# Second mixture of experts in an eight-stage kernel: stationary gate and up weights, brought from DRAM tile by tile

## The chip, the cores and the metric

The kernel runs on one core of one Trainium2 chip. The metric is the device time of one execution in microseconds (us); the time shown for a kernel is the median of its runs. All data are 32-bit floats.

## The reference

Eight layers are added to an activation `x` of 1024 tokens with 256 features, each on a layer norm of the sum so far: an attention, a mixture of experts, a wide attention, a low-rank mixture, a retention, **the second mixture of experts**, a feature attention and a product-key MLP. Only the second mixture (`L2_ffn`) is touched in what it does:

```python
def _moe(x, Wg, W1, W3, W2):            # x: 1024 tokens x 256, 8 experts, hidden 704
    gate_logits = einsum('bsd,de->bse', x, Wg)
    gate_weights = softmax(gate_logits)
    topk_w, topk_idx = top_k(gate_weights, 2)
    topk_w = topk_w / sum(topk_w)
    combine = sum(one_hot(topk_idx, 8) * topk_w[..., None], axis=-2)
    for e in range(8):
        gate = silu(x @ W1[e])           # 256 -> 704
        val = x @ W3[e]                  # 256 -> 704
        out = out + combine[..., e:e+1] * ((gate * val) @ W2[e])   # 704 -> 256
```

## The kernel before

The program is written engine by engine. `MAKERS` gives one stage for each layer, and every engine (SP, POOL, DVE, ACT, PE) runs its part of stage 0, then of stage 1, and so on; semaphores (`after` waits, `tell` signals) order the engines. Nothing is reordered by a compiler, so the order of the lines is the order on each engine. SP issues nearly all transfers, and a wait in its list holds up every transfer behind it. A `_first` function of a stage runs ahead of the `_last` function of the stage before.

`experts(k, l, ...)` makes both mixtures: stage 1 (hidden 176, with a shared expert) and stage 5 (hidden 704, without). `shared_expert` and `LAG` tell them apart. In stage 5:

- **Routing.** PE makes the router's logits (`logits`), DVE turns them into two chosen experts for each token and sorts the 2048 (token, expert) pairs by expert into 23 tiles (`TILES`) of 128 rows; a tile holds rows of one expert alone. DVE first writes one-hot matrices (`hot`, L1018), PE multiplies them into the list of rows (L1238), DVE copies it out (L1020), PE turns it (L1242), DVE writes it as integers, `inv` (L1022). Then DVE makes the two weights of each token (L1025 to L1027) and at last `eid`, the expert of each tile (L1028 to L1030).
- **Weights.** SP loads all eight experts into the big SBUF buffer ahead of the stage: each has 1408 KB of gate and up weights (L890) and 768 KB of down weights (L891), in three groups that wait for the ends of earlier stages (`order`). Engines find a tile's expert by reading `eid` into a register (`place`, L1258).
- **Rows.** POOL gathers the 128 rows of a tile from DRAM with an indirect transfer (`fetch`, L922), four tiles ahead, and scatters the results of a tile to DRAM (`deliver`, L929). `deliver` waits until the scatter before it has landed.
- **A tile.** PE turns its rows (`turn`, L1254: 2 transposes), ACT copies them (L1154), and PE multiplies in `gate_up` (L1269): the turned rows are stationary, the weights stream, in chunks of 352 columns. ACT takes the silu of the gate half (L1162), DVE multiplies by the up half (L1047), PE turns the product (`turn_h`, L1282: 6 transposes), ACT and DVE copy it (L1169, L1053), and PE multiplies with the down weights (`down`, L1293: 6 products of 256 columns); DVE copies the result (L1060). PE shows each f32 product as two MATMUL records with a weight load each (called passes here), each transpose as one: `gate_up` has 16 passes, `down` 12, `turn` 2, `turn_h` 6.

The order on PE in stage 5 for each tile s is

```python
gate_up(s); down(s - 1); turn(s + 1); turn_h(s)
```

When the last `down` has ended, the feature attention (stage 6) begins: its `ready` waits for it, and its SP part (`sp_first`, L2118 and L2120) loads `f_keys` (2048 KB) and `f_tables` (256 KB) while the mixture is still running, after its 8th and its 16th `down`. `sp_last` (L908) then brings the scattered results back, and DVE adds them.

Of the kernel before, what the change touches and what calls it, by code (L numbers as in the profile page):

```python
# [767 lines left out]
def rank_dve(e, ch, k, mask, s, n, ra, rb):  # L768
# [16 lines left out]
            "xg0", "xg1", "xg2", "xg3", "xgt_ps", "xgt_sb", "gu_ps", "hs", "h_sb", "ht_ps", "ht_act", "ht_dve",  # L785
# [3 lines left out]
def experts(k, l, F, chunk, row, base, shared_expert, prefix):  # L789
# [4 lines left out]
    NC = F // chunk  # L794
    NB = -(-F // row)
    FP = NB * row
# [3 lines left out]
    STRIDE = WGU + WD  # L800
    at0, done0 = 8 * l, LOADED + 8 * l
    WB = k.big[:, base:base + E * STRIDE]
    U = Arena(k.big[:, 0:3384], 3384)
# [17 lines left out]
    eq = hot[:, 1, 0:3].rearrange("p t m -> p (t m)")[:, 0:TILES * E].rearrange("p (s e) -> p s e", e=E)  # L821
    A = Arena(k.big[:, low:3384], 3384 - low)
    h1, hh, hT = A.take(F), A.take(FP), A.take(NB, P)
    xgT = [A.take(KB, P) for _ in (0, 1)]
    ys = [A.take(D) for _ in range(YS)]
    if shared_expert:
        A = Arena(k.big[:, 3384:16200], 16200 - 3384)
        ring = A.take(2 * RING, D)
        hT = [hT, A.take(NB, P)]
        FS, FB = 352, (128, 128, 96)  # L830
        sg, sh = [A.take(512) for _ in (0, 1)], A.take(2, len(FB), 512)
        XN = A.take(NT, D)
        shg, shu, shd = k.sh_g, k.sh_u, k.sh_d
    else:
        XN = k.XNT.ap().rearrange("p k t -> p (k t)").rearrange("p (u d) -> p u d", d=D)
        ring = XN
        hT = [hT, hT]
# [38 lines left out]
    def sp(e):  # L876
# [9 lines left out]
        for x, d in order:  # L886
            if d:
                e.wait_ge(k.x_tile, LOADED + 8 * min(d, l))
            w = WB[:, x * STRIDE:(x + 1) * STRIDE]
            tell(e.dma_start(w[:, 0:WGU], g[prefix + "_gu"][x].rearrange("p k f -> p (k f)")), "wts", 16)  # L890
            tell(e.dma_start(w[0:row, WGU:STRIDE].rearrange("p (b d) -> p b d", d=D),  # L891
                             g[prefix + "_d"][x].rearrange("(b p) d -> p b d", p=row)), "wts", 16)
        for t in range(NT):
# [3 lines left out]
            else:  # L897
                tell(e.dma_start(to_xn[t], bc(XN[:, t], 1, 2)), "xn_st", 16)
                if t == 0:
                    tell(e.dma_start(xn_d[0:P], XN[:, 0]), "xn_st", 16)  # L900

# [52 lines left out]
    def dve(e):  # L954
# [69 lines left out]
        for d, w in ((pos[:, 0], wA), (pos[:, 1], wB)):  # L1024
            ch.step(e.tensor_tensor(CN, DM, bc(d, 2, E), ALU.is_equal))  # L1025
            ch.step(e.tensor_tensor(CN, CN, W8, ALU.mult))
            ch.step(e.tensor_reduce(w, CN, AX.X, ALU.add))  # L1027
        ch.step(e.tensor_tensor(eq, bc(bend, 1, TILES), bc(k.slot_no[:, :], 2, E), ALU.is_le))  # L1028
        ch.step(e.tensor_reduce(eidf, eq, AX.X, ALU.add))
        tell(e.tensor_scalar(eid, eidf, E - 1.0, float(STRIDE), ALU.min, ALU.mult), "eid")  # L1030
        after(e, "eid", 1)
        if FP > F:
            ch.step(e.memset(hh[:, F:FP], 0.0))
# [5 lines left out]
        def product(s):  # L1039
            after(e, "hs", s + 1)  # L1040
            if LAG and s >= 1:
                after(e, "ht_ps", s)
            if shared_expert:
                u = k.bank[:, GU[s % 2], F:2 * F]
                ins = e.tensor_tensor(hh, h1, u, ALU.mult)
            else:
                ins = e.tensor_tensor(hh[:, 0:F].rearrange("p (n c) -> p n c", n=NC),  # L1047
                                      h1.rearrange("p (n c) -> p n c", n=NC), k.bank[:, NC:2 * NC, 0:chunk], ALU.mult)
            tell(ins, "h_sb")

        def turned(s):
            after(e, "ht_ps", s + 1)
            tell(e.tensor_copy(hT[s % 2][:, 4:NB], k.bank[:, HT[0] + 1, 0:(NB - 4) * P]  # L1053
                               .rearrange("p (b m) -> p b m", m=P)), "ht_dve")
# [7 lines left out]
        for s in range(TILES):  # L1062
# [3 lines left out]
            if NB > 4:  # L1066
                turned(s)
# [64 lines left out]
    def act(e):  # L1132
# [23 lines left out]
        def gate(s):  # L1156
# [3 lines left out]
            src = k.bank[:, GU[s % 2], 0:F] if shared_expert else k.bank[:, 0:NC, 0:chunk]  # L1160
            dst = h1 if shared_expert else h1.rearrange("p (n c) -> p n c", n=NC)
            tell(e.activation(dst, src, ACT.Silu), "hs")  # L1162

        def turned(s):
            after(e, "ht_ps", s + 1)
            if s >= 1 + LAG:
                after(e, "y_ps", s - LAG)
            n = min(NB, 4)
            tell(e.copy(hT[s % 2][0:row, 0:n], k.bank[0:row, HT[s % 2], 0:n * P].rearrange("p (b m) -> p b m", m=P)),  # L1169
                 "ht_act")  # L1170
# [7 lines left out]
        if LAG:  # L1178
            rows(1)
        for s in range(TILES + LAG):  # L1180
            if s < TILES:
                gate(s)
            if s + 1 < TILES and not LAG:
                rows(s + 1)
            if s >= LAG:
                turned(s - LAG)
            if s + 2 < TILES and LAG:
# [6 lines left out]
    def pe(e):  # L1194
# [54 lines left out]
        def turn(s):  # L1249
            after(e, f"xg{s % RING}", 16 * (s // RING + 1))  # L1250
            if s >= 2 or (s >= 1 and not LAG):
# [5 lines left out]
        def place(s):  # L1257
            at[s] = e.value_load(eid[0:1, s:s + 1], min_val=0, max_val=(E - 1) * STRIDE)  # L1258

        def gate_up(s):  # L1260
            after(e, "xgt_sb", s + 1)
            if s >= 1 + LAG:
                after(e, "h_sb", s - LAG)
            elif shared_expert:
                after(e, "shy", NT - 1 + s)
            for c in range(2 * NC):
                out = bank[:, GU[s % 2], c * F:(c + 1) * F] if shared_expert else bank[:, c, 0:chunk]
                for kb in range(KB):
                    ins = e.matmul(out, xgT[s % 2][:, kb, :], WB[:, bass.ds(at[s] + (kb * 2 * F + c * chunk), chunk)],  # L1269
                                   start=kb == 0, stop=kb == KB - 1)  # L1270
                if c == 0 and s + 1 < TILES:
                    place(s + 1)
            tell(ins, "gu_ps")

        def turn_h(s):
            after(e, "h_sb", s + 1)
            if s >= 1 + LAG:
                after(e, "ht_act", s - LAG)
                if NB > 4:
                    after(e, "ht_dve", s - LAG)  # L1280
            for b in range(NB):
                ins = e.transpose(bank[0:row, HT[s % 2] + b // 4, b % 4 * P:(b % 4 + 1) * P], hh[:, b * row:(b + 1) * row],  # L1282
                                  k.ident[:, :])
            tell(ins, "ht_ps")

        def down(s):
            after(e, "ht_act", s + 1)
            if NB > 4:
                after(e, "ht_dve", s + 1)
            if s >= 1 + LAG:  # L1290
                after(e, "y_sb", s - LAG)
            for b in range(NB):
                ins = e.matmul(bank[:, Y[s % 2], 0:D], hT[s % 2][0:row, b, :],  # L1293
                               WB[0:row, bass.ds(at[s] + (WGU + b * D), D)], start=b == 0, stop=b == NB - 1)
# [1724 lines left out]
```

## Time and profile before

| | |
|---|---|
| median of 3 runs | 1110.07 us (1109.78 to 1110.41) |
| the profiled execution's own time | 1108.07 us |
| its span, first to last instruction | 1106.3 us |
| mean granted TensorE clock | 0.952 of full speed |
| PE busy | 1004.5 us, 91% of the span |
| DVE, ACT, POOL busy | 567.0, 367.5, 265.8 us |
| read from and written to DRAM | 54.72 MB, 11.40 MB |

The second mixture takes the stretch from about 566 to 805 us; its 23 tiles run from about 601 to 798 us. A busy PE means that passes are in flight, not that the array is at its peak: the time from the start of one group of passes to the start of the next is the better measure. Idle time of an engine that nobody waits for costs nothing.

### The profile page before, as it was taken

To read this page: it belongs to the slowest core of one execution; us is meant where nothing else is said; L and a number is where in the kernel's file an instruction comes from. 1 tells how busy PE (TensorE), PEld (TensorE's weight loads), DVE (VectorE), ACT (ScalarE), POOL (GpSimd) and SP (SyncE) were. 2 spreads that over 40 slices of the span, in tenths; PEclk is the share of its full clock that TensorE was granted. 3 is DMA by queue.
4 is the path that set the end of the run, shared out by engine and by line. 5 is a ranking of instruction groups with operands and counts; after the bars stand their busy time and mean duration, and the time that the engine had idled before them with its cause. 6 is when DMAs were issued, how large, how long until landed. Compare 5 with 4: busy or idle time off the path is not lost.

```text
span 1106.3 us, 17644 instructions
## 1 busy us (share of the span) xinstructions
PE 1004.5 (91%) x6722; PEld 667.7 (60%) x6722; DVE 567.0 (51%) x1286; ACT 367.5 (33%) x687; POOL 265.8 (24%) x336
## 2 busy tenths in 40 slices
PE   5888999989999999978865999999869999997989
PEld 4766599546766766667653777777623443453467
DVE  5877433455435435465474221221267878556792
ACT  3653133242122122214210222221114666745660
POOL 4431342410000000031521122221252344202350
PEclk9996999999999999989976999999958999998999
DMA  9103033211101100192054013011012200020000
GB/s 286 36 2 105 9 97 91 83 57 30 38 16 39 37 27 11 34 361 82 1 217 130 20 34 110 30 43 29 20 60 76 101 1 1 2 76 0 1 10 29
DMA packets 37432, 67.25 MB, mean 61 GB/s; under 512 B 4456, under 2 KB 27080, under 8 KB 35816
## 3 DMA queue, kind: packets, MB, share of 16 engines
q1 hardware_dynamic: 29960, 51.98, 13.9%
q0 software_dynamic: 4080, 11.15, 3.5%
q10 hardware_dynamic: 3312, 3.02, 0.8%
q8 instruction: 56, 0.92, 0.3%
q14 instruction: 24, 0.20, 0.1%
HBM read 54.72 MB, written 11.40 MB: 60 GB/s over the span
## 4 chain that ended last, share of the span: by engine, by line
PE 74%; DVE 13%; ACT 5%; DMA 3%; issue 2%; POOL 2%; SPq 0%; DVEq 0%; ACTq 0%; POOLq 0%
PE bank L354 21%; PE bank L1269 13%; PE bank L1293 7%; PE bank L1619 5%; PE bank L2341 5%; PE bank L2366 3%; PE bank L2387 3%; PE bank L1282 2%; PE bank L2836 2%; PE bank L1630 2%; PE bank L1595 2%; PE bank L2405 1%; DVE big L2623 1%; DVE big L2196 1%; ACT big L563 1%
## 5 line engine op out<-in xcount | busy, mean ns | idle before, releaser
L1269 PE MATMUL bank<-big 128*128 x552 | 147.7, 417 | 0.6 <-ACT big L1154 0.6
L354 PE MATMUL bank<-XNT,big 128*128 128x512 f32 x296 | 136.5, 609 | 6.9 <-DVE big L2576 5.4
L1269 PEld LDWEIGHTS bank<-big 128*128 128x128 f32 x552 | 98.1, 191 | 39.5 <-issue 2.3
L270 POOL TENSOR_TENSOR rstd<-ve,half 128x1 f32<-128x1 f32 x48 | 27.8, 582 | 302.7 <-DVE ve L264 302.6
L2341 PE MATMUL bank<-big,xs 32*128 32x512 f32 x256 | 89.8, 738 | 11.7 <-DVE xs L281 10.2
L354 PEld LDWEIGHTS bank<-XNT,big 128*128 128x128 f32 x296 | 55.1, 194 | 69.8 <-issue 59.1
L2196 DVE TENSOR_REDUCE big<-bank 128x2 f32<-128x512 f32 x128 | 81.9, 685 | 21.2 <-PE bank L2341 20.4
L1293 PE MATMUL bank<-big 128*128 (+1 forms) x368 | 87.2, 380 | 1.1 <-ACT big L1169 1.1
L1047 DVE TENSOR_TENSOR big<-big,bank 128x704 f32<-128x704 f32 x23 | 20.4, 889 | 124.7 <-ACT big L1162 124.7
L2287 ACT ACTIVATE big<-bank 128x1024 f32<-128x1024 f32 x64 | 64.9, 1024 | 40.2 <-PE bank L2366 39.9
L354 PE MATMUL bank<-CTXT,big 128*128 128x512 f32 (+1 forms) x192 | 67.3, 495 | 10.7 <-DMA big<-wvT 10.7
L1293 PEld LDWEIGHTS bank<-big 128*128 128x128 f32 (+1 forms) x368 | 68.0, 190 | 13.6 <-issue 1.7
L2366 PE MATMUL bank<-big 32*128 32x512 f32 x256 | 69.4, 666 | 1.4 <-POOL big L2141 1.2
L1162 ACT ACTIVATE big<-bank 128x176 f32<-128x176 f32 (+1 forms) x46 | 24.8, 538 | 136.6 <-PE bank L1269 136.6
L1619 PE MATMUL bank<-big 128*128 128x256 f32 x256 | 63.5, 393 | 1.5 <-issue 1.2
L929 POOL DMA_INDIRECT yg<-big x23 | 22.7, 986 | 150.6 <-DVE big L1060 150.6
L354 PEld LDWEIGHTS bank<-CTXT,big 128*128 128x128 f32 x192 | 33.3, 199 | 40.9 <-issue 40.8
L354 PE MATMUL bank<-big,CTXT 128*128 128x256 f32 (+1 forms) x224 | 58.0, 409 | 0.0
L1478 DVE COPY big<-bank 128x512 f32<-128x512 f32 x16 | 11.1, 691 | 88.9 <-PE bank L1604 88.9
L1526 ACT COPY big<-bank 128x1024 f32<-128x1024 f32 x16 | 16.2, 1013 | 119.1 <-PE bank L1630 119.1
L1619 PEld LDWEIGHTS bank<-big 128*128 128x128 f32 x256 | 47.0, 194 | 13.5 <-DVE X L1472 5.8
L2341 PEld LDWEIGHTS bank<-big,xs 32*128 32x128 f32 x256 | 32.0, 209 | 34.7 <-issue 18.8
(350 smaller groups left out, 1758.6 us busy)
## 6 DMA issues: line engine op xcount, KB each, us to landing
big<-m_gu SPq DMA_DIRECT2D x8, 1408.0 KB
big<-m_d SPq DMA_DIRECT2D x8, 768.0 KB
big<-a_qk SPq DMA_DIRECT2D x16, 256.0 KB, 3.0
yg<-big ACTq DMA_DIRECT2D x23, 128.0 KB, 2.0
big<-m_gu SPq DMA_DIRECT2D x8, 352.0 KB
big<-a_o SPq DMA_DIRECT2D x16, 128.0 KB, 2.1
xn<-XNT SPq DMA_DIRECT2D x8, 256.0 KB, 7.1
big<-f_keys SPq DMA_DIRECT2D x1, 2048.0 KB, 8.3
```

What stands on the lines that cost most here:

```text
L270: e.tensor_tensor(k.rstd[at % NT][:, :], k.ve[at % NT][:, :], k.half[:, 0:1], ALU.pow).then_inc(k.ln_rstd, 1)
L354: ins = e.matmul(out, a, b, start=start and n == 0, stop=stop and n == len(pairs) - 1)
L929: tell(e.indirect_dma_start(yg_d, bass.IndirectOffsetOnAxis(ap=inv[:, s:s + 1], axis=0), ys[s % YS], None), f"dv{s % YS}", 16)
L1162: tell(e.activation(dst, src, ACT.Silu), "hs")
L1269: ins = e.matmul(out, xgT[s % 2][:, kb, :], WB[:, bass.ds(at[s] + (kb * 2 * F + c * chunk), chunk)], start=kb == 0, stop=kb == KB - 1)
L1293: ins = e.matmul(bank[:, Y[s % 2], 0:D], hT[s % 2][0:row, b, :], WB[0:row, bass.ds(at[s] + (WGU + b * D), D)], start=b == 0, stop=b == NB - 1)
L1619: ins = e.matmul(bank[:, QK0 + j % 2, q * D:(q + 1) * D], cT[:, t * P:(t + 1) * P], wo[h % 2], start=True, stop=True)
L2196: e.tensor_reduce(nm[t % 2][:, b, c:c + 2 * G:G], k.bank[:, step_bank(step), :].rearrange("p (j n) -> p j n", j=2), AX.X, ALU.max, negate= ...
L2287: e.activation(pt[u % 2][:, r].rearrange("p r j n -> p r (j n)"), k.bank[:, b:b + 2, :], ACT.Exp, scale=float(G) ** -0.5).then_inc(S["ex"], 1)
L2341: e.matmul(bank[:, step_bank(step), :], k.xs[t % 2][q, b * P:(b + 1) * P], cm[t % 2][q, 2 * jp:2 * jp + 2].rearrange("p j n -> p (j n)"), ...
L2366: ins = e.matmul(bank[:, pair_banks(u, pair) + r % 2, :], cr[q, t, jp, nb * P:(nb + 1) * P], xm[t % 2][q, 2 * jp:2 * jp + 2].rearrange("p ...
L2387: ins = e.matmul(bank[r * R:(r + 1) * R, VB, jp * D:(jp + 1) * D], cv[t % 2][:, nb, r * J + 2 * jp + j], pt[u % 2][:, r, j], start=nb == 0 ...
```

## The change

For stage 5 alone:

1. **Operands change places.** In `gate_up` a block of 128 weight columns is now stationary and the turned rows (128 columns) stream: 11 blocks with 2 products each, 44 passes of 128 columns in place of 16 of 352. The output comes out already turned (hidden features on partitions). `turn_h` and the two copies behind it (L1169, L1053) are gone in this stage; silu writes `h1` and the product goes straight into `hT`. The hidden size 704 is five blocks of 128 and a half: the sixth block holds the last 64 gate columns and the last 64 up columns, so silu and product each become two instructions (640 and 128 elements a partition; the second on 64 partitions). `hT` has two buffers, and the half block of `hT` that nothing writes is cleared once. The host lays out `m5_gu` and `m5_d` to match.
2. **A transfer for each tile.** The gate and up weights aren't loaded ahead any more. SP reads `eid` for each tile into a register and loads that expert's 1408 KB into one of three slots: 23 transfers in place of 8. The load of tile 1 waits for the gather of tile 1; from tile 3 on, a load waits for the end of the `gate_up` three tiles back.
3. **Down weights.** All eight (768 KB each) are loaded after one wait, for the end of stage 2, in place of three groups that wait for stages 1, 2 and 4.
4. **Order.** On PE a tile becomes `gate_up(s); down(s - 1); turn(s + 2)`, with two turned tiles made ahead of the loop and two sets of three PSUM banks for `gate_up`.
5. **Expert table.** DVE makes `eid` and the two token weights between the one-hot matrices and the copy of the list of rows, not behind it. This is done in both mixtures.
6. SP's load of `f_keys` and `f_tables` stands behind the 23 new transfers in SP's list.

```diff
-    h1, hh, hT = A.take(F), A.take(FP), A.take(NB, P)
+    if shared_expert:
+        h1, hh = A.take(F), A.take(F)
+    else:
+        h1 = A.take(WHOLE, P)
+    hT = [A.take(NB, P) for _ in (0, 1)]
...
-        GU, HT, Y, XT = (0, 0), (4, 4), (6, 6), (7, 7)
+        GU, Y, XT = (0, 3), (6, 6), (7, 7)
...
+    def gates_up(s):
+        b = GU[s % 2]
+        return k.bank[:, b:b + 3, :].rearrange("p b (n m) -> p (b n) m", m=P)
...
-        order = [(x, 0) for x in range(E)] if shared_expert else \
-            [(x, d) for d, group in ((2, (3, 4)), (3, (1, 2, 5)), (5, (0, 6, 7))) for x in group]
+        if not shared_expert:
+            e.wait_ge(k.x_tile, LOADED + 8 * min(3, l))
...
+        if shared_expert:
+            return
+        after(e, "eid", 1)
+        for s in range(TILES):
+            x = e.value_load(eid[0:1, s:s + 1], min_val=0, max_val=E - 1)
+            if s == 1:
+                after(e, "xg1", 16)
+            if s >= SLOTS:
+                after(e, "gu_ps", s - SLOTS + 1)
+            tell(e.dma_start(gu_slot[s % SLOTS], g[prefix + "_gu"][bass.ds(x, 1)].rearrange("x p k f -> p (x k f)")),
+                 f"gl{s % SLOTS}", 16)
...
         for q in (0, 1):
             tell(e.tensor_tensor(hot[:, q], bc(pr[:, q], 2, P), bc(k.row_no[:, :], 1, NT), ALU.is_equal), "hot")
+        ch.step(e.tensor_tensor(eq, bc(bend, 1, TILES), bc(k.slot_no[:, :], 2, E), ALU.is_le))
+        ch.step(e.tensor_reduce(eidf, eq, AX.X, ALU.add))
+        tell(e.tensor_scalar(eid, eidf, E - 1.0, float(STRIDE) if shared_expert else 1.0, ALU.min, ALU.mult), "eid")
+        for d, w in ((pos[:, 0], wA), (pos[:, 1], wB)):
...
         after(e, "inv_ps", 1)
...
+                gu, rest = gates_up(s), hT[s % 2][P - PART:P, WHOLE]
+                e.tensor_tensor(hT[s % 2][:, 0:WHOLE], h1, gu[:, 12 - WHOLE:12], ALU.mult)
+                tell(e.tensor_tensor(rest, rest, gu[P - PART:P, WHOLE], ALU.mult), "h_sb")
...
+                e.activation(h1, gu[:, 0:WHOLE], ACT.Silu)
+                tell(e.activation(hT[s % 2][P - PART:P, WHOLE], gu[0:PART, WHOLE], ACT.Silu), "hs")
...
         def gate_up(s):
             after(e, "xgt_sb", s + 1)
-            if s >= 1 + LAG:
-                after(e, "h_sb", s - LAG)
+            if s >= 2:
+                after(e, "h_sb", s - 1)
...
+                gu = gates_up(s)
+                after(e, f"gl{s % SLOTS}", 16 * (s // SLOTS + 1))
+                for n in range(2 * F // P):
+                    for kb in range(KB):
+                        c = kb * 2 * F + n * P
+                        ins = e.matmul(gu[:, n if n <= WHOLE else n + 1], gu_slot[s % SLOTS][:, c:c + P],
+                                       xgT[s % 2][:, kb, :], start=kb == 0, stop=kb == KB - 1)
+                    if n == 0 and s + 1 < TILES:
+                        place(s + 1)
...
         if not shared_expert:
             turn(0)
+            turn(1)
         for s in range(TILES + 1 + LAG):
...
-            if s + 1 + LAG < TILES:
-                turn(s + 1 + LAG)
-            if not LAG and s < TILES:
-                turn_h(s)
+            if s + 2 < TILES:
+                turn(s + 2)
```

## Rows read from the trace of the kernel before

**Rows 1.** The page: busy time, granted clock in 40 slices of 27.7 us.

```profile
PE 1004.5 (91%) x6722; PEld 667.7 (60%) x6722; DVE 567.0 (51%) x1286; ACT 367.5 (33%) x687; POOL 265.8 (24%) x336
...
PEclk9996999999999999989976999999958999998999
```

**Rows 2.** PE's waits, 600 to 800 us: total us, times, longest.

```profile
PE bank L1254 <- DMA XNT<-xn,big: 3.6, 1, 3.6
PE bank L1282 <- DVE big L1047: 1.6, 1, 1.6
```

**Rows 3.** Timeline of one tile: start us, us, engine, line, what.

```profile
619.21 5.00 PE L1269 MATMUL bank<-big 128*128 x16
...
624.04 2.75 PE L1293 MATMUL bank<-big 128*128 x12
624.25 0.76 ACT L1162 ACTIVATE big<-bank 128x704 f32<-128x704 f32 x1 [4.30 <-PE bank L1269]
625.04 0.89 DVE L1047 TENSOR_TENSOR big<-big,bank 128x704 f32<-128x704 f32 x1 [5.26 <-ACT big L1162]
...
626.63 0.38 PE L1254 MATMUL bank<-ident,XNT 128*128 128x128 f32 x2
...
626.85 0.82 PE L1282 MATMUL bank<-ident,big 128*128 128x128 f32 x6
...
627.57 5.00 PE L1269 MATMUL bank<-big 128*128 x16
```

**Rows 4.** Timeline of PE in the low-rank mixture: 64 passes of 128 columns.

```profile
502.36 0.61 PE L1785 MATMUL bank<-CTXT,big 128*128 128x128 f32 x4
...
504.15 0.71 PE L1785 MATMUL bank<-CTXT,big 128*128 128x128 f32 x4
504.70 0.61 PE L1787 MATMUL bank<-big,CTXT 128*128 128x128 f32 x4
...
509.83 0.38 PE L1795 MATMUL bank<-ident,big 128*128 128x128 f32 x2
```

**Rows 5.** Windows: busy us of engines, granted clock, DMA share, GB/s.

```profile
601.70:605.30 3.60, 3.59 (x7) 2.13 (x8) 0.00 (x0) 1.17 (x1) 1.63 (x2) 0.53 0.44 109
...
620.00:780.00 160.00, 160.00 (x690) 118.16 (x689) 33.03 (x57) 32.64 (x57) 36.44 (x38) 1.00 0.15 47
```

**Rows 6.** Timeline of the mixture's start, 596 to 611 us.

```profile
596.47 0.28 DVE L1020 COPY big<-bank 23x128 f32<-23x128 f32 x1 [4.73 <-PE bank L1238]
...
597.17 0.22 DVE L1025 TENSOR_TENSOR big<-big 128x64 f32<-128x64 f32 x1
...
598.90 0.99 POOL L922 DMA_INDIRECT XNT<-xn,big  x1 [0.30 <-issue]
...
599.48 0.40 DVE L1030 TENSOR_SCALAR big<-big 128x23 int32<-128x23 f32 x1
...
600.67 0.43 PE L1254 MATMUL bank<-ident,XNT 128*128 128x128 f32 x2 [3.63 <-DMA XNT<-xn,big]
...
601.71 6.69 PE L1269 MATMUL bank<-big 128*128 x16 [0.60 <-ACT big L1154]
...
610.96 4.90 PE L1269 MATMUL bank<-big 128*128 x16
```

**Rows 7.** Transfers: one load of 2048 KB, a window inside it, gathers beside it.

```profile
big<-f_keys SPq DMA_DIRECT2D x1, 2048.0 KB, 8.3
...
680.00:683.00 3.00, 3.00 (x13) 2.00 (x12) 0.00 (x0) 0.28 (x1) 0.00 (x0) 1.00 0.99 416
...
DMA to landing us min/median/max: 3.1/4.8/6.4
```

**Rows 8.** Timeline of the last tile: the last `down`, the last scatter.

```profile
795.28 2.85 PE L1293 MATMUL bank<-big 128*128 x12 [0.76 <-ACT big L1169]
...
798.87 0.97 POOL L929 DMA_INDIRECT yg<-big  x1 [3.30 <-DVE big L1060]
```

**Rows 9.** Line 1258 on PE's sequencer: reading `eid`, ns min/median/max.

```profile
L1258 PEldq TENSOR_LOAD <-big x46: 297/300/485, 140.1 to 778.1; - x46
```

More of the change, by code:

```diff
@@ L799, in experts @@
     WGU, WD = KB * 2 * F, NB * D
-    STRIDE = WGU + WD
+    STRIDE = WD + WGU * shared_expert
     at0, done0 = 8 * l, LOADED + 8 * l
     WB = k.big[:, base:base + E * STRIDE]
+    SLOTS = 3
+    gu_slot = [k.big[:, base + E * WD + q * WGU:base + E * WD + (q + 1) * WGU] for q in range(SLOTS)]
     U = Arena(k.big[:, 0:3384], 3384)
@@ L828, in experts @@
         ring = A.take(2 * RING, D)
-        hT = [hT, A.take(NB, P)]
         FS, FB = 352, (128, 128, 96)
@@ L883, in sp @@
             tell(e.dma_start(gw, g[prefix + "_gate"]), "gate_ld", 16)
[L884 to L888 removed]
+        if not shared_expert:
+            e.wait_ge(k.x_tile, LOADED + 8 * min(3, l))
+        for x in range(E):
             w = WB[:, x * STRIDE:(x + 1) * STRIDE]
[L890 to L891 removed]
+            if shared_expert:
+                tell(e.dma_start(w[:, 0:WGU], g[prefix + "_gu"][x].rearrange("p k f -> p (k f)")), "wts", 16)
+            tell(e.dma_start(w[0:row, STRIDE - WD:STRIDE].rearrange("p (b d) -> p b d", d=D),
                              g[prefix + "_d"][x].rearrange("(b p) d -> p b d", p=row)), "wts", 16)
@@ L1022, in dve @@
         tell(e.tensor_copy(inv, k.bank[:, INV, P:P + TILES]), "inv")
[L1024 to L1033, printed above, removed]
+        if not shared_expert:
+            for p in (0, 1):
+                ch.step(e.memset(hT[p][0:PART, WHOLE], 0.0))
         if shared_expert:
@@ L1040, in product @@
             after(e, "hs", s + 1)
-            if LAG and s >= 1:
-                after(e, "ht_ps", s)
             if shared_expert:
-                u = k.bank[:, GU[s % 2], F:2 * F]
-                ins = e.tensor_tensor(hh, h1, u, ALU.mult)
-            else:
[L1047 to L1054, printed above, removed]
+                if s >= 1:
+                    after(e, "ht_ps", s)
+                tell(e.tensor_tensor(hh, h1, k.bank[:, GU[s % 2], F:2 * F], ALU.mult), "h_sb")
+            else:
+                gu, rest = gates_up(s), hT[s % 2][P - PART:P, WHOLE]
+                e.tensor_tensor(hT[s % 2][:, 0:WHOLE], h1, gu[:, 12 - WHOLE:12], ALU.mult)
+                tell(e.tensor_tensor(rest, rest, gu[P - PART:P, WHOLE], ALU.mult), "h_sb")
         def result(s):
@@ L1159, in gate @@
                 after(e, "h_sb", s)
-            src = k.bank[:, GU[s % 2], 0:F] if shared_expert else k.bank[:, 0:NC, 0:chunk]
-            dst = h1 if shared_expert else h1.rearrange("p (n c) -> p n c", n=NC)
-            tell(e.activation(dst, src, ACT.Silu), "hs")
+            if shared_expert:
+                tell(e.activation(h1, k.bank[:, GU[s % 2], 0:F], ACT.Silu), "hs")
+            else:
+                gu = gates_up(s)
+                e.activation(h1, gu[:, 0:WHOLE], ACT.Silu)
+                tell(e.activation(hT[s % 2][P - PART:P, WHOLE], gu[0:PART, WHOLE], ACT.Silu), "hs")
         def turned(s):
             after(e, "ht_ps", s + 1)
-            if s >= 1 + LAG:
[L1167 to L1170, printed above, removed]
+            if s >= 2:
+                after(e, "y_ps", s - 1)
+            tell(e.copy(hT[s % 2][0:row], k.bank[0:row, HT[s % 2], 0:NB * P].rearrange("p (b m) -> p b m", m=P)), "ht_act")
         def store(s):
@@ L1177, in act @@
         rows(0)
-        if LAG:
-            rows(1)
+        rows(1)
         for s in range(TILES + LAG):
@@ L1182, in act @@
                 gate(s)
[L1183 to L1187, printed above, removed]
+            if LAG and s >= 1:
+                turned(s - 1)
+            if s + 2 < TILES:
                 rows(s + 2)
@@ L1250, in turn @@
             after(e, f"xg{s % RING}", 16 * (s // RING + 1))
-            if s >= 2 or (s >= 1 and not LAG):
+            if s >= 1 + LAG:
                 after(e, "xgt_sb", s - LAG)
```

71 lines of the change are left out of this document (36 added, 35 removed).

## The prediction

> **What bounds the kernel now.** I read the page first: PE is busy in 91% of the span [rows 1], so the question is what PE does in the stretch that is changed. PE's waits there come next. Over the 200 us of the mixture's tiles they are four, with 6.6 us together; the two longest stand in [rows 2], and all lie in the first and the last tile. The window from 620 to 780 us says the same: 160.00 of 160 us busy, granted clock 1.00, DMA engines busy in 0.15 of the time, DVE 33 us, ACT 33 us, POOL 36 us [rows 5]. PE alone sets the pace, and every other engine and the transfers have wide room. The timeline of one tile then prices PE's work by the distance of starts [rows 3]: `gate_up` 619.21 to 624.04, 4.83 us; `down` 2.59 us; `turn` 0.22 us; `turn_h` 0.72 us; 8.36 us a tile, 23 times.
>
> **The operands change places.** `turn_h` goes: 0.72 us a tile. The copies behind it go from ACT and DVE, which had idle time anyway, so they give nothing by themselves. `gate_up` keeps its product of columns and passes (16 x 352 = 44 x 128 = 5632), but needs 44 weight loads in place of 16, each hidden only behind a pass of 128 columns. The nearest rows are the 64 passes of the low-rank mixture, with a new 128x128 stationary operand at each and 128 streamed columns [rows 4]. From 502.36 to 504.15 are 16 passes: 0.112 us each. Over all 64, to 509.83, it is 0.117 us. The difference is holes of 0.10 us: the group at 504.15 takes 0.55 us to the next start where the others take 0.45. Such a hole is one pass whose weight load stood exposed because PE had just been released from a wait. I take 0.112, as the new order lets every wait of a tile be met long before (below): 44 x 0.112 = 4.92 us, so `gate_up` costs 0.09 us more than now. Bounds: 0.117 us gives 5.13, and 0.107 us (16 passes of 352 columns in 4.83 us, by column) gives 4.72.
>
> The new tile is 4.92 + 2.59 + 0.22 = 7.73 us, 0.63 us less. The clock stays at its higher level, 2.4 GHz, in this loop, since PE has even fewer gaps.
>
> **Trainium skill against this row.** The page "TensorE: Matmul & The Clock Gate", section "Measured speedup vs the span model", says that a weight load overlaps passes in flight only when it goes to another row group; here all 128 rows are used by every pass. By that rule each of the 44 loads would stand exposed: a tile of about 12.1 us and a time near 1197. The trace disagrees: an exposed load costs 0.10 us [rows 4], and most of the 64 passes show none.
>
> **Silu and product** become two instructions each. They took 0.76 and 0.89 us for 704 elements [rows 3]. If each of the four took as long as the old one, the chain would be 3.3 us; by size I take 2.4 us from the end of `gate_up` to `h_sb`. Until `down(s)` stand `down(s-1)`, `turn` and `gate_up(s+1)` on PE, 7.7 us, so it is hidden; only in the last tile is the cover no more than one `down`, 2.59 us. There I take 0, at worst 1.0 us. All the other waits (`xgt_sb`, `y_sb`, the second `gate_up` bank set) were met a tile before.
>
> **Reading `eid` on PE** stays once a tile, but now behind 4 passes of 0.112 us, not of 0.30 us. It takes 0.30 us for the load [rows 9] and some 0.2 for what follows. If PE's sequencer runs ahead of the array, which nothing now stops at `gate_up`'s head, it is hidden. If not, it costs some 0.15 us and an exposed load of 0.10 in each tile: 5.8 us in all. I take 0 and keep 5.8 for the range.
>
> **A load for each tile.** The row for a load is `f_keys`: 2048 KB landed after 8.3 us, at 416 GB/s inside [rows 7]. By size that is 5.7 us for 1408 KB; with all but the transfer itself fixed it is 3.5 + 3.3 = 6.8 us. A load is issued when `gate_up` of three tiles back ends, so it has `down`, `turn` and two more tiles, over 15 us, with two loads in flight. By traffic a tile needs 1.44 MB of weights and about 0.26 MB of gather and scatter: 1.70 MB at 416 GB/s is 4.1 us of 7.73. Hidden, price 0. The tile before did not get longer beside `f_keys`: the window inside it has PE busy 3.00 of 3 us [rows 7]. Gathers are slower beside such a load: 6.4 us where 3.1 is the least [rows 7]. They are issued two tiles or more ahead, and `deliver` waits for the scatter before it, 7.7 us back: still enough.
>
> **The start.** DVE now makes the token weights and `eid` in the 4.73 us in which it waits for PE's list product [rows 6]. They are nine small instructions from 597.17 to 599.88 [rows 6], 2.7 us, so 2.0 us of the cover stay unused and the list of rows is not delayed. Were the cover gone, the whole 2.7 us would be on the path. PE's list product lets DVE go on at 596.47, so DVE is free from 591.74; the three steps of `eid`, up to 0.40 us each, come first, and `eid` stands at 591.74 + 1.2 = 592.9, SP reads it (0.5 us), and load 0 lands at 593.4 + 5.7 to 6.8 = 599.1 to 600.2. It isn't late: gather 0 lands at 600.67. PE now turns tile 1 too before `gate_up(0)`. Its gather starts at 598.90, lands at about 602.0 with 3.1 us, and `gate_up(0)` starts at 602.2, 0.5 us later than now. The start runs at granted clock 0.53 [rows 5], near the lower level, 1.2 GHz; that costs the first `gate_up` 6.69 - 5.00 = 1.69 us now [rows 3, 6], and the same columns will pay the same: 4.92 + 1.69 = 6.6, until 608.8, with `turn(2)` 609.0. Load 1, issued at 602.0 to 602.5, lands at 607.7 to 609.3: 0 to 0.3 us of stall, taken as 0. The second `gate_up` starts at 609.0 where it now starts at 610.96 [rows 6]: the 1.6 us wait of tile 0 for DVE [rows 2] is gone.
>
> **Sum.** From 609.0: 22 `gate_up` of 4.92 = 108.2; 23 `down` of 2.59 = 59.6; 20 `turn` of 0.22 = 4.4; the drain of the last pass 0.16. The last `down` ends at 781.4. It now ends at 798.13 [rows 8]. The gain is 16.7 us.
>
> **What is moved past what.** `f_keys` now stands behind load 22, which waits for `gate_up(19)`. From there to the last `down` are three tiles and 5.3 us, 28 us; load 22 and `f_keys` need about 3.5 + 8.3 = 12 us and `f_tables` little more. Price 0; with under 12 us left it would be paid in full by POOL, whose first key product stands behind the last scatter. The down weights, now 6.3 MB at the end of stage 2, are first used at 615 us. The 6.6 MB before the routing go; nobody on the path waits for them, since POOL waited for the list of rows. The last scatter starts 0.74 us behind the last `down` [rows 8] and all behind it shifts with it. In the first mixture `eid` and the weights only move in DVE's order, and PE is full there: 0, at most 1 us either way.
>
> 16.7 us less 0.2 for the stall at load 1: 16.5 us. The profiled execution took 1108.07 us (span 1106.3 and 1.8 around it) and would take 1091.6; the median of the runs lies 2.0 us above it, so I predict 1093.6.
>
> **Rivals.**
> - *Exposed weight loads; slower.* If in `gate_up` the loads are not pulled ahead, a pass takes 0.112 + 0.10 = 0.21 us, the tile 12.1 us, and the time is 1110 + 23 x 3.8 = about 1197. For it: 44 loads in a row from freshly written memory have no row. Against it: [rows 4]. It decides from 0.126 us a pass, where 44 passes eat up `turn_h`. It is also what the skill's rule of row groups would do here. Chance 0.04.
> - *The loads set the pace; slower.* If 23 loads with a register in their address, beside gathers and scatters, move at under 204 GB/s (1.70 MB in 8.36 us), PE waits in every tile. At half of 416 it is 8.2 us a tile, and nothing much is gained; at 180 GB/s it is 9.4 us and the time 1134. Against it: 416 GB/s beside a full PE. Chance of slower 0.03, of within 0.2% 0.03.
> - *Holes in the tile; less gain.* The `eid` read or waits met late expose 0.25 us a tile, or passes at 0.117 us cost 4.8: 1098.5 to 1099.5. Chance 0.12.
> - *A late start; less gain.* Gathers 0 and 1 are held up by load 0 as `f_keys` held one (6.4 us, not 3.1), or load 1 comes late: 3 to 4 us, 1097 to 1098. Chance 0.10.
> - *My forecast*, 1091 to 1096: 0.68.
>
> **Numbers.** The low end is the forecast with 0.107 us passes limited to half of their 5 us: 1091. The high end takes all holes and 1.5 us of the start: 1101. The range leaves out about 0.1. About 0.2% (2.2 us) is what a measurement here can tell from no change. Faster 0.90, same 0.03, slower 0.07.
>
> **What the profile after will show.** Right: 44 passes of L1269's successor in 4.9 us, no transposes of the product, tiles 7.7 us apart, PE's waits in the loop empty, loads landing in 6 to 7 us, the last `down` near 781. Wrong: idle in front of `gate_up` released by a transfer (the loads), distances of 0.12 us or more between passes (weight loads, `eid` reads), `gate_up(0)` starting after 603 (gathers), stage 6 waiting for `f_keys`.

## The result

The changed kernel takes 1093.04 us (median of 4 runs, 1091.83 to 1095.84) against 1109.92 us for the kernel before in the same sessions. The ratio is 0.986, 95% interval 0.9846 to 0.9875: 16.9 us less. The forecast was 1093.6 us, 1091 to 1101. The profiled execution took 1094.08 us, with a span of 1092.2 us; it is one of the slower ones and that of before (1108.07) one of the faster, so its span is 14.1 us below that of before and not 16.9.

The page of the changed kernel: the lines that answer to [rows 1], the passes and weight loads of `gate_up` (busy us, mean ns, idle time before them), and two transfers (KB each, us to landing):

```profile
PE 992.6 (91%) x7228; PEld 696.5 (64%) x7228; DVE 562.6 (52%) x1287; ACT 358.9 (33%) x687; POOL 266.2 (24%) x336
...
PEclk9995999999999999989985999999968999999999
...
L1289 PE MATMUL bank<-big 128*128 128x128 f32 x1012 | 118.4, 276 | 0.0
L1289 PEld LDWEIGHTS bank<-big 128*128 128x128 f32 x1012 | 116.4, 194 | 0.3 <-issue 0.2
...
big<-m_gu SPq DMA_DIRECT2D x23, 1408.0 KB, 6.2
...
big<-f_keys SPq DMA_DIRECT2D x1, 2048.0 KB, 10.8
```

The 1012 passes are 23 times 44. Weight loads are busy for 116.4 us of the 118.4 us of the passes: each has hardly more than its own pass to hide in, and nobody waits for them. One tile in the timeline of the changed kernel, as [rows 3]:

```profile
618.10 5.08 PE L1289 MATMUL bank<-big 128*128 128x128 f32 x44
...
623.01 2.76 PE L1308 MATMUL bank<-big 128*128 x12
623.21 0.70 ACT L1176 ACTIVATE big<-bank 128x640 f32<-128x640 f32 x1 [4.54 <-PE bank L1289]
623.93 0.27 ACT L1177 ACTIVATE big<-bank 64x128 f32<-64x128 f32 x1
624.23 0.82 DVE L1067 TENSOR_TENSOR big<-big,bank 128x640 f32<-128x640 f32 x1 [5.72 <-ACT big L1177]
625.07 0.29 DVE L1068 TENSOR_TENSOR big<-big,bank 64x128 f32<-64x128 f32 x1
...
625.61 0.38 PE L1264 MATMUL bank<-ident,XNT 128*128 128x128 f32 x2
...
625.82 5.08 PE L1289 MATMUL bank<-big 128*128 128x128 f32 x44
```

By the distances of starts, `gate_up` is 4.91, `down` 2.60 and `turn` 0.21 us; the tile is 7.72 us, where it was 8.36 [rows 3]. Windows of the changed kernel, as [rows 5]:

```profile
603.00:606.00 3.00, 2.82 (x14) 2.85 (x15) 0.00 (x0) 1.69 (x3) 1.55 (x2) 0.50 0.74 171
606.00:609.00 3.00, 3.00 (x27) 3.00 (x27) 0.00 (x0) 0.00 (x0) 0.00 (x0) 0.95 1.01 416
620.00:770.00 150.00, 150.00 (x1133) 143.16 (x1132) 29.26 (x57) 25.60 (x58) 36.23 (x37) 1.00 0.64 225
```

PE is busy 150.00 of 150 us, with DMA engines now busy in 0.64 of the time, not 0.15. The timeline at the start and the end of the mixture, as [rows 6] and [rows 8]:

```profile
597.72 0.28 DVE L1047 COPY big<-bank 23x128 f32<-23x128 f32 x1 [2.48 <-PE bank L1248]
...
602.13 0.44 PE L1264 MATMUL bank<-ident,XNT 128*128 128x128 f32 x2 [3.83 <-DMA XNT<-xn,big]
...
603.63 6.37 PE L1289 MATMUL bank<-big 128*128 128x128 f32 x44
...
610.06 5.39 PE L1289 MATMUL bank<-big 128*128 128x128 f32 x44
...
780.76 2.85 PE L1308 MATMUL bank<-big 128*128 x12 [0.73 <-DVE big L1074]
...
784.65 0.97 POOL L949 DMA_INDIRECT yg<-big  x1 [2.91 <-DVE big L1074]
```

One number is used from here on, **the stretch**: from the start of DVE's copy of the list of rows to the end of the last `down`. Executions differ in what lies ahead of it (here the copy came 1.25 us later than in [rows 6]; over all profiled runs of this document it came between 595.6 and 600.0 us) and in what lies behind it (305.8 to 309.8 us); the stretch carries neither. Before it is 798.13 - 596.47 = 201.7 us [rows 6, 8]; now it is 783.61 - 597.72 = 185.9 us, 15.8 us less.

### The profile page after: what moved, and what is told of

Read it like the earlier page. It is cut to its first block, busy times and chain, and to the rows that moved or that the text cites. A ratio compares the mean times of both kernels' runs of the same rounds, so it can differ in the third digit from the quotient of the medians.

```text
span 1092.2 us, 18562 instructions
## 1 busy us (share of the span) xinstructions
PE 992.6 (91%) x7228; PEld 696.5 (64%) x7228; DVE 562.6 (52%) x1287; ACT 358.9 (33%) x687; POOL 266.2 (24%) x336
## 4 chain that ended last, share of the span: by engine, by line
PE 74%; DVE 13%; ACT 5%; DMA 3%; issue 2%; POOL 2%; SPq 0%; DVEq 0%; ACTq 0%; POOLq 0%
PE bank L354 21%; PE bank L1289 10%; PE bank L1308 7%; PE bank L1633 6%; PE bank L2355 5%; PE bank L2380 3%; PE bank L2401 3%; PE bank L2850 3%; PE bank L1279 3%; PE bank L1644 2%; PE bank L1609 2%; PE bank L2419 1%; PE bank L2856 1%; DVE big L2210 1%; PE bank L1264 1%
## 5 line engine op out<-in xcount | busy, mean ns | idle before, releaser
L1289 PE MATMUL bank<-big 128*128 128x128 f32 x1012 | 118.4, 276 | 0.0
L1289 PEld LDWEIGHTS bank<-big 128*128 128x128 f32 x1012 | 116.4, 194 | 0.3 <-issue 0.2
L270 POOL TENSOR_TENSOR rstd<-ve,half 128x1 f32<-128x1 f32 x48 | 27.7, 581 | 302.9 <-DVE ve L264 302.7
L2355 PE MATMUL bank<-big,xs 32*128 32x512 f32 x256 | 88.9, 732 | 12.4 <-DVE xs L281 10.6
L1067 DVE TENSOR_TENSOR big<-big,bank 128x640 f32<-128x640 f32 x23 | 18.9, 822 | 136.5 <-ACT big L1177 136.5
L1633 PEld LDWEIGHTS bank<-big 128*128 128x128 f32 x256 | 47.0, 194 | 13.6 <-DVE X L1486 5.7
L1540 ACT COPY big<-bank 128x1024 f32<-128x1024 f32 x16 | 16.2, 1012 | 119.1 <-PE bank L1644 119.1
L354 PEld LDWEIGHTS bank<-big,CTXT 128*128 128x128 f32 x224 | 42.5, 190 | 17.3 <-issue 12.9
## 6 DMA issues: line engine op xcount, KB each, us to landing
big<-f_keys SPq DMA_DIRECT2D x1, 2048.0 KB, 10.8
```

What stands on the lines that cost most here:

```text
L270: e.tensor_tensor(k.rstd[at % NT][:, :], k.ve[at % NT][:, :], k.half[:, 0:1], ALU.pow).then_inc(k.ln_rstd, 1)
L354: ins = e.matmul(out, a, b, start=start and n == 0, stop=stop and n == len(pairs) - 1)
L1289: ins = e.matmul(gu[:, n if n <= WHOLE else n + 1], gu_slot[s % SLOTS][:, c:c + P], xgT[s % 2][:, kb, :], start=kb == 0, stop=kb == KB - 1)
L1633: ins = e.matmul(bank[:, QK0 + j % 2, q * D:(q + 1) * D], cT[:, t * P:(t + 1) * P], wo[h % 2], start=True, stop=True)
L2355: e.matmul(bank[:, step_bank(step), :], k.xs[t % 2][q, b * P:(b + 1) * P], cm[t % 2][q, 2 * jp:2 * jp + 2].rearrange("p j n -> p (j n)"), ...
```

## Experiments

Each ratio is against runs of the kernel before on the same chip in the same session. A cut in an edit is marked with three dots.

**The changed kernel again.** No edit.

> The changed kernel, timed again as the base for the others. 1093 us, tiles 7.73 us apart, the last down 186 us behind the copy of the list of rows. If the gain were an accident of one profile, the stretch from the copy of the list to the last down would differ from 185.9 us by more than 1 us.

1093.37 us, ratio 0.9857 (0.9841 to 0.9872); stretch 185.9 us, as expected. This is the base for the rest.

**Rows turned one tile ahead.**

```diff
             turn(0)
-            turn(1)
...
-            if s + 2 < TILES:
-                turn(s + 2)
+            if s + 1 + LAG < TILES:
+                turn(s + 1 + LAG)
```

(The same in ACT's `rows`.)

> Rows are turned one tile ahead, as before the change, and not two. Theory: the gain is 0.72 us of product transposes less 0.09 us, but those transposes also hid ACT's copy of the turned rows; without two tiles ahead, PE waits at the head of each gate_up for turn, copy and a cold weight load, about 0.7 to 0.8 us a tile. Tiles 8.4 to 8.5 us apart, total about 1109 us: nearly the whole gain gone, from one change of order. Rival: the order is of no matter, since PE's queue hides a wait of 0.7 us, and the gain comes from the operands alone: tiles 7.73 us apart, 1093 us.

1111.89 us, ratio 1.0045 (1.0029 to 1.0061): the whole gain is gone, and a little more. The timeline of PE, its weight loads and ACT in this kernel:

```profile
660.59 0.38 PE L1265 MATMUL bank<-ident,XNT 128*128 128x128 f32 x2
...
661.01 0.37 ACT L1166 COPY big<-bank 128x256 f32<-128x256 f32 x1 [1.82 <-PE bank L1265]
661.43 0.52 PEld L1290 LDWEIGHTS bank<-big 128*128 128x128 f32 x4 [0.70 <-ACT big L1166]
661.43 5.41 PE L1290 MATMUL bank<-big 128*128 128x128 f32 x44 [0.46 <-ACT big L1166]
...
662.11 4.54 PEld L1290 LDWEIGHTS bank<-big 128*128 128x128 f32 x40 [0.15 <-issue]
```

From `turn` at 660.59 to `gate_up` at 661.43 are 0.84 us; without the 0.21 us that `turn` needs, 0.63 are a wait for ACT's copy. `turn_h` had filled just this time [rows 3]. The tile before began `gate_up` at 652.69, so this tile is 8.74 us (others 8.65 to 8.75): 7.72 + 0.63, and 0.4 us more that the theory had only in part. 0.1 of it is the first weight load of `gate_up`, which stands exposed behind the wait. Behind the fourth weight load stands a gap of its own, 0.15 us here. Its cause is the next run.

**The same, with `eid` read later.** The edit is against the run with one tile ahead.

```diff
-                    if n == 0 and s + 1 < TILES:
+                    if n == 5 and s + 1 < TILES:
                         place(s + 1)
```

> The kernel with one tile ahead, turn behind down, in which eid is read behind the 6th block of 128 columns of gate_up and not behind the first. Theory: there PE is released from a wait at the head of gate_up, so its sequencer is only 4 passes ahead of the array when it stands still for the read (0.5 us), and that is the gap of 0.15 to 0.21 us before the fifth weight load; 24 passes later the sequencer is far ahead and the gap is gone: tiles 8.44 to 8.5 us apart in place of 8.7, 5 us less than with the early read, 1106 to 1107 us. Rival: the gap comes from somewhere else (the head of gate_up itself): tiles stay at 8.7 us, 1111 to 1112 us.

1110.71 us (1107.92 to 1113.1), ratio 1.0009 (0.9998 to 1.002). Tiles are 8.45 us apart, and the gap behind the fourth load is gone in the timeline of PE:

```profile
662.13 0.38 PE L1265 MATMUL bank<-ident,XNT 128*128 128x128 f32 x2
...
662.98 4.99 PEld L1290 LDWEIGHTS bank<-big 128*128 128x128 f32 x44 [0.70 <-ACT big L1166]
662.98 5.18 PE L1290 MATMUL bank<-big 128*128 128x128 f32 x44 [0.46 <-ACT big L1166]
```

The stretch is 202.4 us, with the early read 207.6: 5.2 us less, as expected. The whole time is not as expected (1106 to 1107 us): the medians differ by only 1.2 us. The two runs come from different sessions; the ratios, each against its own, differ by 0.0036 or 4.0 us, and their intervals don't meet. In the two profiled executions the list's copy came 3.0 us later and the part behind the last `down` took 2.0 us longer with the late read, which the edit doesn't touch; that is the spread named above. So the read of `eid` costs 0.2 to 0.3 us a tile if it comes within 4 short passes of a wait that has just ended. Behind 24 passes it costs nothing that can be seen: `gate_up` takes 5.01 us, which is the 4.91 of the base and the one exposed load.

**One tile ahead, `turn` in front of `down`.** The edit is against the run with one tile ahead; `eid` is read early, as there.

```diff
+            if s + 1 + LAG < TILES:
+                turn(s + 1 + LAG)
             if not LAG and s >= 1:
                 down(s - 1)
-            if s + 1 + LAG < TILES:
-                turn(s + 1 + LAG)
```

> One tile ahead as in the run with one tile ahead, but turn(s+1) stands before down(s-1), not behind it. Theory: what matters is that work of PE covers ACT's copy of the turned rows, not that two tiles are ahead: down (2.59 us) covers it, tiles 7.73 us apart again, 1093 us within 1.5 us; only gate_up(1), which has no down before it, waits. Rival: the second tile ahead is what gives the gain (the read of eid and the waits need it): tiles 8.0 us or more apart, 1100 us or more.

1095.26 us (1090.68 to 1097.04), ratio 0.9865 (0.9846 to 0.9883). Tiles 7.72 us apart; the stretch is 187.3 us, 1.4 more, of which 1.25 are the wait of `gate_up(1)`. The median is 0.8 us above the expected range, within the spread of its runs. Cover for the copy is what counts, not the second tile ahead.

**No loads after the third.** Tiles 3 to 22 compute with the weights of the first three slots.

```diff
-        for s in range(TILES):
+        for s in range(SLOTS):
             x = e.value_load(eid[0:1, s:s + 1], min_val=0, max_val=E - 1)
...
-                after(e, f"gl{s % SLOTS}", 16 * (s // SLOTS + 1))
+                after(e, f"gl{s % SLOTS}", 16)
```

> Loads 3 to 22 are left out: every tile computes with the weights of one of the first three slots, so the output is not the mixture's. Theory: the loads are hidden, PE sets the pace: tiles 7.73 us apart as with the loads, 1093 us within 1.5 us. Rival: the 229 GB/s of loads beside PE cost it something (slower reads of the stationary operands, late gathers): without them the tiles come closer, to 7.6 us or less, and the time falls by 3 us or more.

1092.48 us, ratio 0.986 (0.984 to 0.988). Tiles 7.72 us apart, stretch 185.8 us. Twenty transfers of 1408 KB cost nothing that can be measured: the rival falls. (Loads 0 to 2 are still there, so this run says nothing of the start.)

**One slot.** `SLOTS = 1`.

> One slot for the gate and up weights in place of three: a load starts only when the gate_up before it has ended. Theory: the load (6.2 us to landing, 0.4 us to issue) stands behind gate_up with nothing but down and turn, 2.8 us, beside it: a tile of 4.92 + 6.6 = 11.5 us, 3.8 us more, 22 times; 1093 + 83 = 1176 us if the clock holds in the 3.8 us gaps, and up to 1230 if it falls to the lower level. Rival: a lone load lands in much less than the 6.2 us it shows in a stream (1408 KB at 416 GB/s are 3.5 us): tile under 9.5 us, 1130 us.

1214.59 us, ratio 1.0957 (1.0926 to 1.0988). PE's waits in this kernel:

```profile
PE bank L1289 <- DMA big<-m_gu: 79.2, 22, 5.9
```

Its timeline on PE, one tile:

```profile
665.05 7.02 PE L1289 MATMUL bank<-big 128*128 128x128 f32 x44 [3.26 <-DMA big<-m_gu]
671.90 2.75 PE L1308 MATMUL bank<-big 128*128 x12
674.49 0.38 PE L1264 MATMUL bank<-ident,XNT 128*128 128x128 f32 x2
...
678.57 1.68 PE L1289 MATMUL bank<-big 128*128 128x128 f32 x7 [3.70 <-DMA big<-m_gu]
```

And windows over the gap and the `gate_up` behind it, and in the last two lines over the gap and the `gate_up` of the tile before (granted clock, DMA share and GB/s last):

```profile
661.50:665.00 3.50, 0.28 (x3) 0.04 (x1) 0.42 (x1) 0.37 (x1) 1.96 (x2) 1.00 0.84 350
665.00:668.00 3.00, 2.95 (x15) 2.82 (x16) 0.00 (x0) 0.00 (x0) 0.00 (x0) 0.63 0.20 44
668.00:672.00 4.00, 4.00 (x32) 4.00 (x32) 0.00 (x0) 0.00 (x0) 0.00 (x0) 0.85 0.02 4
...
650.00:653.50 3.50, 0.27 (x3) 0.03 (x1) 0.42 (x1) 0.37 (x1) 1.96 (x2) 1.00 0.83 350
653.58:656.58 3.00, 3.00 (x25) 2.83 (x26) 0.00 (x0) 0.00 (x0) 0.00 (x0) 1.00 0.17 44
```

The total lies inside the expected 1176 to 1230 us. A lone load still takes 5.9 us to land, so the rival falls. The tile shown is 13.5 us: 3.7 of wait, as expected, and 1.9 more in `gate_up` (6.85 us, not 4.91). Of these, 1.6 us go with a lower granted clock (0.63, then 0.85), and 0.3 us are the exposed read of `eid`. Three tiles tell the two apart: in `gate_up` of tiles 4, 11 and 19, behind waits of 3.3, 3.3 and 3.5 us, the clock stayed at 1.00, and it took 5.23 us. In the other tiles from 1 to 21 it took 6.8 us or more, behind waits from 3.2 us on. So a gap of this length was mostly, but not each time, followed by the lower clock, and its length doesn't tell which. The mean of the tiles is 13.1 us.

**Twice the traffic.** Two slots, and a second load of the same weights into the third, which nobody reads.

```diff
-    SLOTS = 3
+    SLOTS = 2
...
+            if s >= 1:
+                e.wait_ge(again_ld, 16 * s)
+            e.dma_start(gu_slot[SLOTS], g[prefix + "_gu"][bass.ds(x, 1)].rearrange("x p k f -> p (x k f)"))\
+                .then_inc(again_ld, 16)
+        e.wait_ge(again_ld, 16 * TILES)
```

> Two slots, and each load is followed by a second one of the same 1408 KB into the third slot, which nobody reads; it waits for the one before it. 3.1 MB a tile in place of 1.7. Theory: at 416 GB/s that is 7.5 us of 7.73, so PE still sets the pace or loses little: tiles 7.7 to 8.1 us apart, 1093 to 1102 us. Rival (the loads set the pace from some rate on, well under 416 GB/s in a stream with gathers and scatters): at 300 GB/s a tile takes 10.4 us, 1155 us.

1104.63 us, ratio 0.9957 (0.9944 to 0.9971): 11 us more than the base, 2.6 above the theory's range and far from the rival's 1155. Transfers move 383 GB/s. The stretch is 199.3 us, 13.4 more. Gathers and scatters land in 6.4 us, not in 3.2 and 3.4, and `gate_up(1)` starts 2.9 us later behind the list's copy. The other 10.5 us are in the tiles: PE waits for loads four times, 4.2 us together; in eight tiles `gate_up` is released late and takes 5.2 to 5.3 us, the exposed read of `eid`, where it takes 4.91 us otherwise (2.7 us together); behind the longest wait, 2.3 us, `gate_up` took 6.6 us, at a granted clock of 0.50 in its first 3 us (1.7 us). The rest, some 2 us, are shorter waits. PE's waits of this kernel:

```profile
PE bank L1296 <- DMA big<-m_gu: 4.2, 4, 2.3
```

and two windows, of 60 us and of the 3 us behind the longest wait, granted clock, DMA share and GB/s last:

```profile
640.00:700.00 60.00, 58.47 (x430) 54.55 (x429) 10.78 (x21) 9.92 (x22) 13.74 (x14) 1.00 0.99 383
...
736.27:739.27 3.00, 3.00 (x14) 3.00 (x15) 0.00 (x0) 0.00 (x0) 0.53 (x1) 0.50 0.98 407
```

**Load 1 at once**, without its wait for the gather of tile 1.

```diff
-            if s == 1:
-                after(e, "xg1", 16)
```

> Load 1 no longer waits for the gather of tile 1; loads 0, 1 and 2 stand in the queue behind each other from 594.8 us. Theory: a gather that runs beside a load lands when the load does, as the gather beside f_keys did (6.4 us); three loads end at about 606, so gather 0 lands at 605 to 606 and not at 602.1, and the start is 3 to 4 us later: 1096 to 1097 us. Rival: gathers and loads share the engines packet by packet, a gather is at most 1 us later, and load 1 comes earlier: 1092 to 1094 us.

1096.80 us, ratio 0.9893 (0.9872 to 0.9913). Gather 0, issued at 598.16, lands at 604.2 and gather 1 at 606.1; without the edit they take 3.3 and 3.0 us. The stretch is 189.1 us, 3.2 more. The late-start rival of the prediction is real as soon as loads 1 and 2 stand behind load 0, and it is the wait for `xg1` that keeps it away. Load 1 is early here, and `gate_up(1)` takes 4.91 us. The timeline of PE at the start:

```profile
604.22 0.69 PE L1262 MATMUL bank<-ident,XNT 128*128 128x128 f32 x2 [6.56 <-DMA XNT<-xn,big]
...
606.15 0.69 PE L1262 MATMUL bank<-ident,XNT 128*128 128x128 f32 x2 [1.25 <-DMA XNT<-xn,big]
606.63 6.30 PE L1287 MATMUL bank<-big 128*128 128x128 f32 x44
```

**The table late**, in the second mixture alone: the block of `eid` and the token weights behind `inv`, as before.

```diff
         tell(e.tensor_copy(inv, k.bank[:, INV, P:P + TILES]), "inv")
+        if not shared_expert:
+            weights()
+            table()
```

> In the second mixture the token weights and the expert table are made behind the list of rows again. Theory: the table comes at about 601 us of the trace instead of 593.8, load 0 is issued at 602 and lands 6.2 us later, at 608; the first gate_up starts at 608 instead of 603.6, and all behind it shifts: 4 to 5 us more, 1097 to 1098 us. Rival: the start is set by the gathers and by tile 1's load alone, and only the part of load 0 beyond 603.6 that load 1 would have cost anyway counts: under 1 us, 1093 to 1094 us.

1103.07 us, ratio 0.995 (0.9937 to 0.9963): 9.7 us more than the base, twice what the theory gave. The stretch is 194.7 us, 8.8 more. The timeline at the start, SP's issue of load 0 and the first `gate_up`:

```profile
600.99 30.39 SPq L919 DMA_DIRECT2D big<-m_gu  x6
...
610.36 7.47 PEld L1299 LDWEIGHTS bank<-big 128*128 128x128 f32 x44 [8.24 <-issue]
610.39 7.63 PE L1299 MATMUL bank<-big 128*128 128x128 f32 x44 [7.87 <-DMA big<-m_gu]
```

Load 0 was issued at 601.0, 1 us earlier than foreseen, but took 9.3 us to land, not 6.2: loads 1 and 2 followed 1.1 and 2.3 us later, and the gathers of tiles 1 to 4 ran beside them. The gathers make the difference: in the run with load 1 at once, load 0 had the same two loads 1.1 and 2.3 us behind it, but no gather until 598.2 us, and it landed after 5.7 us. The window from 603 to 605 us, with three gathers in flight, has the DMA engines busy in 0.84 of the time at 140 GB/s, the one from 605 to 607 at 395 GB/s:

```profile
603.00:605.00 2.00, 0.00 (x0) 0.00 (x0) 0.00 (x0) 1.23 (x1) 0.78 (x1) 0.50 0.84 140
605.00:607.00 2.00, 0.00 (x0) 0.00 (x0) 0.00 (x0) 0.00 (x0) 0.00 (x0) 0.50 0.96 395
```

And after a wait of 7.9 us the first `gate_up` took 7.6 us, 1.3 us more. Both were missing in the theory.

**The table alone**: the kernel before with the table's move. The edit is against the kernel before; the same lines behind `inv` are taken out, and `eq` gets a buffer of its own, as in the changed kernel.

```diff
...
+        ch.step(e.tensor_tensor(eq, bc(bend, 1, TILES), bc(k.slot_no[:, :], 2, E), ALU.is_le))
+        ch.step(e.tensor_reduce(eidf, eq, AX.X, ALU.add))
+        tell(e.tensor_scalar(eid, eidf, E - 1.0, float(STRIDE), ALU.min, ALU.mult), "eid")
...
         after(e, "inv_ps", 1)
```

> The kernel before, with the move of the table alone (both mixtures). Theory: PE waits for gather 0, not for the table, so nothing changes: 1110 us within 1 us, tiles 8.36 us apart. Rival: the 2.7 us of DVE work stood on the path in one of the two mixtures, and up to 2.7 us of the gain belong to the move: 1107 us.

1109.29 us, ratio 1.0006 (0.9998 to 1.0015), stretch 201.7 us: no change.

**Head and tail.**

```diff
+                    if n == 6 and s == 0:
+                        turn(1)
...
-                after(e, "xg1", 16)
+                after(e, "xg0", 16)
...
-                ins = e.matmul(bank[:, Y[s % 2], 0:D],
+                ins = e.matmul(bank[:, Y[s % 2] if s < last else 3, 0:D],
```

> The changed kernel with three edits: turn(1) stands inside gate_up(0), behind its 7th block; load 1 waits for the gather of tile 0, not of tile 1; and the last down writes a bank of gate_up's other set, so it need not wait for DVE's copy of the result before it. Theory: gate_up(0) starts 0.7 us earlier and load 1 lands 1 us earlier, the last down starts 0.8 us earlier: the stretch from the copy of the list to the last down is 1.6 to 1.9 us shorter than 185.9 us, 1091 to 1092 us. Rival: a wait of the same size comes back at once (load 1 still late, the first gate_up in the slower clock for longer, the last scatter behind the one before it): the stretch shrinks by under 0.8 us, 1093 us.

1093.49 us, ratio 0.9854 (0.984 to 0.9868). The rival holds. The last `down` has no wait left, but `gate_up(1)` still waits for load 1 (0.2 us) and starts 12.75 us behind the copy of the list, where the base run's start was 12.4; the last scatter waits for the one before it. The stretch is 185.3 us, 0.6 less, and the scatter isn't earlier at all: it starts 3.88 us behind the one before it, just as in the base run, though its input is ready 1.0 us earlier in the time between the two. So in the changed kernel, too, it is the scatter before that holds it, although the profile names DVE there. Its row in the timeline, 187.3 us behind the list's copy (186.9 in the base run):

```profile
784.75 0.97 POOL L950 DMA_INDIRECT yg<-big  x1 [2.91 <-DMA yg<-big]
```

No version beats the changed kernel by more than the runs can tell.

## Why the prediction was right, step by step

- **Passes.** 0.112 us was forecast from [rows 4]; 44 take 4.91 us, 0.1116 us each. The lower bound was worked out wrongly: 16 passes of 352 columns in 4.83 us are 0.110 us for 128 columns, not 0.107, and 44 of them 4.83 us, not 4.72. Only the low end of the range hung on it. The rival of exposed weight loads did not happen, nor does the Trainium skill's rule of row groups (page "TensorE: Matmul & The Clock Gate"), as the prediction quoted it, hold for these passes: every load goes to the row group in use, and 1012 loads gave 0.3 us of idle time in all. What the prediction quoted stands on that page of the Trainium skill, in the section "The mechanism", as a rule for matmuls packed side by side; the same section lets a load also run ahead when it goes to a background weight buffer, and the trace, in which loads run beside passes of the same row group, agrees with that.
- **Tile.** 7.73 us forecast, 7.72 measured. The argument that waits are met early was right and carried more than was seen: the sum took `turn_h`'s 0.72 us as a plain gain, while that time also covered a copy. The run with one tile ahead shows that without the new order nothing would have been gained.
- **Silu and product.** 2.4 us forecast; in the last tile from 777.28 to 779.62, 2.34 us.
- **Loads.** 5.7 to 6.8 us forecast, 6.2 measured (median; 5.9 to 9.3); price 0, confirmed for the loop by the run without them. The traffic forecast (4.1 of 7.72 us) was low: the DMA share is 0.64, 4.9 us.
- **Start.** Load 0 was issued at 594.8, 0.98 us after `eid`, where 0.5 us was forecast; it didn't matter. Counted from the list's copy, `gate_up(0)` came at 5.9 us (forecast 5.7) and the second at 12.3 (forecast 12.5); the lower clock cost the first 1.3 us, not 1.69. Load 1 was issued at 603.0 and landed at 609.9, just in front of `gate_up(1)`, which then took 5.23 us at a granted clock of 1.00: the exposed read of `eid` once, 0.3 us. In the two runs in which load 1 landed well ahead of it (load 1 at once, the table late) `gate_up(2)` followed 7.72 us behind `gate_up(1)`, not 8.04.
- **End.** The term that was mis-sized: the last `down` was to start right behind the one before it. It waits 0.73 us for DVE's copy of the result, since there is one PSUM bank for results, and 0.1 us for its first weight load. Before, `turn_h` of the last tile stood there. It is the second place where the transposes had hidden something. Without it and the 0.3 us of `gate_up(1)` the sum is right to 0.3 us: forecast 16.7, measured 15.8. A second argument on the end was wrong: the scatter before the last was to be 7.7 us back, but the last two are 3.9 us apart, since no `gate_up` stands between the last two `down`. So the last scatter starts 1.04 us behind the last `down`, where it was 0.74 [rows 8], and up to there the gain is 15.5 us.
- **Moves.** `f_keys` took 10.8 us behind the last loads and landed at 765.8, 19 us ahead of the last scatter. The table's move alone gives 0; with the loads behind it, it is worth 9.7 us.
- **Median.** 16.9 us in the medians against 15.8 in the stretch: the rest is put down to spread, since ahead of the stretch and behind it executions differ by 4 us. That the 6.6 MB less to load ahead of the routing, or the first mixture, give a part of it was not tested on the changed kernel; the table's move alone, which is in both mixtures, gave nothing. That the forecast of 1093.6 us met the median of 1093.04 to 0.6 us is luck in part: of the 16.5 us forecast the stretch gave 0.7 us less, and 1.1 us came from outside it.

## What to carry to other kernels

When work is taken from the engine that bounds the kernel, look up what else ran while it ran: here six transposes of 0.72 us had covered a copy for which PE otherwise waits 0.63 us and, in the last tile, another for which it waits 0.73. An edit that removes cover needs an order that gives it back: without that order this one gained nothing. A transfer per tile was free with the DMA engines busy in 0.64 of the time and cost 11 us with 0.99. Small transfers on which the start hangs must be kept out of the way of large ones.

## What the runs showed of the hardware

- A register read on PE's sequencer (0.30 us and what follows it) costs 0.2 to 0.3 us when it stands 4 short passes behind a wait that has just ended, and nothing that can be seen 24 passes behind it, or where no wait is near.
- A load of 1408 KB lands after 5.9 us alone. With two more issued 1.1 and 2.3 us behind it, the first of three still landed after 5.7 us, and the others after 8.2 and 12.0. With four gathers beside the same three, they took 9.3, 11.7 and 13.9 us. A gather beside two or three loads takes 6 us and more, not 3.
- After 3.2 to 5.9 us of waiting, with only two transposes close in front of it, PE's passes ran at the lower granted clock for some us in 18 of the 21 tiles from 1 to 21 (0.63 over 3 us and 0.85 over the next 4 in the one shown): 1.6 us a tile, on top of the wait. In three tiles, behind 3.3, 3.3 and 3.5 us, the clock stayed at 1.00. In the run with twice the traffic it fell to 0.50 behind a wait of 2.3 us.
- 44 passes of 128 f32 columns take 4.91 us with transfers at 383 GB/s beside them (tiles without a late release in the run with twice the traffic) as well as without any.
